# Four graph layers on one core: chunk 0's graph attention woven into the attention iterations, and another order of work at both ends

## The reference

```python
x = x + attention0(h, adj)        # 8 heads of 32, softmax over the neighbours, with biases
x = x + attention1(h, adj)        # the same without biases in q, k, v; o + layernorm(o) * gamma + beta
x = x + graph_attention(h, adj)   # hw = h W; e = leaky(s1_i + s2_j) * adj; softmax; elu(att hw + beta hw)
x = x + recurrence(h, adj)        # three steps of a gated unit:
#   a = adj h; z = sigmoid(a W3 + h U3); r = sigmoid(a W4 + h U3)
#   hv = tanh(a W5 + (r h) U5); h = (1 - z) h + z hv
```

## Time and profile before

| | us |
|---|---|
| median of 3 runs | 1524.75 (1520.08 to 1526.09) |
| the profiled execution, its own time | 1525.95 |
| its span in the trace | 1524.2 |
| TensorE busy | 1463.7 |
| VectorE busy | 1244.6 |
| ScalarE busy | 991.5 |
| GpSimd busy | 534.8 |

### The profile page before, as it was taken

One profiled execution on the slowest core, in us unless ns is written; L12 is line 12 of the kernel. 1 busy time (PEld: TensorE's weight loads), 2 busy tenths in 40 slices (PEclk: granted clock), 3 DMA queues, 4 the chain that ended last, 5 costly groups with the idle time before them and its releaser, 6 DMA issues.

```text
span 1524.2 us, 45691 instructions
## 1 busy us (share of the span) xinstructions
PE 1463.7 (96%) x18840; PEld 1233.9 (81%) x18840; DVE 1244.6 (82%) x2510; ACT 991.5 (65%) x1792; POOL 534.8 (35%) x622
## 2 busy tenths in 40 slices
PE   5899999899899998799999999999999999999997
PEld 4789989799798887588888888888888887888885
DVE  4777888888899999788888788888888888888676
ACT  4666667577677776666666666666666666666553
POOL 2676777567777887411111111111101111111000
PEclk9999999999999999899999999999999999999998
DMA  8200000012322235100000000000000000000000
GB/s 263 85 3 0 0 0 1 7 26 44 58 55 55 55 64 78 29 1 1 29 2 2 30 1 1 30 1 1 30 1 1 30 1 1 29 2 1 29 1 28
DMA packets 36827, 40.96 MB, mean 27 GB/s; under 512 B 11856, under 2 KB 31824, under 8 KB 36688
## 3 DMA queue, kind: packets, MB, share of 16 engines
q0 software_dynamic: 4608, 16.78, 5.9%
q1 hardware_dynamic: 32080, 22.10, 4.9%
HBM read 13.71 MB, written 8.39 MB: 14 GB/s over the span
## 4 chain that ended last, share of the span: by engine, by line
PE 87%; DVE 7%; POOL 2%; ACT 2%; issue 2%; DMA 0%; DVEq 0%; POOLq 0%; ACTq 0%
PE ring L99 40%; PE scores L99 27%; PE scores L1589 3%; PE ring L1408 3%; PE scores L1372 2%; PE ring L1448 2%; PE ring L1629 2%; PE ring L1419 1%; PE ring L1573 1%; PE ring L1701 1%; PE ring L1531 1%; POOL s L534 1%; PE ring L1542 1%; DVE total L993 1%; DVE stats L955 1%
## 5 line engine op out<-in xcount | busy, mean ns | idle before, releaser
L534 POOL TENSOR_TENSOR s<-s,mx 128x512 f32<-128x512 f32 x128 | 137.4, 1092 | 49.4 <-DVE mx L989 49.4
L540 POOL TENSOR_TENSOR s<-s,rtotal 128x512 f32<-128x512 f32 x128 | 131.4, 1064 | 35.9 <-DVE rtotal L995 35.7
L600 POOL TENSOR_TENSOR r_var_eps<-r_mean_var,eps 128x4 f32<-128x4 f32 x16 | 8.1, 509 | 377.1 <-DVE r_mean_var L1146 377.1
L684 ACT ACTIVATE s<-s 128x512 f32<-128x512 f32 x128 | 78.3, 643 | 75.1 <-POOL s L534 75.1
L1275 DVE TENSOR_TENSOR rhp_lo<-r,rhp_hi 128x1024 fp32r<-128x1024 f32 x48 | 58.8, 1226 | 72.8 <-ACT rhp_hi L865 72.8
L984 DVE SCALAR_TENSOR_TENSOR s<-scores,mask 128x512 f32<-128x512 f32 x128 | 87.2, 681 | 35.4 <-PE scores L1372 35.4
L884 ACT ACTIVATE hv<-scores,bias 128x512 f32<-128x512 f32 x96 | 66.2, 689 | 58.0 <-PE scores L99 58.0
L847 ACT ACTIVATE r<-r,bias_half 128x512 f32<-128x512 f32 x96 | 64.4, 717 | 59.6 <-DVE r L1249 59.6
L858 ACT ACTIVATE later_w<-ring 128x512 f32<-128x512 f32 x64 | 34.8, 595 | 99.9 <-PE ring L1629 99.9
L696 ACT ACTIVATE pT<-ring 128x512 f32<-128x512 f32 x128 | 66.1, 602 | 45.4 <-PE ring L1408 45.4
L989 DVE TENSOR_REDUCE mx<-s 128x8 f32<-128x512 f32 x128 | 87.9, 686 | 4.4
(11 more groups left out here) (288 smaller groups left out, 5108.6 us busy)
## 6 DMA issues: line engine op xcount, KB each, us to landing
x<-beta_less_one POOLq DMA_DIRECT2D x16, 512.0 KB, 4.7
x<-o POOLq DMA_DIRECT2D x16, 512.0 KB, 6.6
...
```

The source lines that it names most:

```text
L534: pool.tensor_tensor(sr, sr, mx[:, r, :].unsqueeze(2).to_broadcast([P, CT * 2, N]), ALU.subtract).then_inc(s_shifted, 1)
L540: pool.tensor_tensor(sr, sr, rtotal[:, r, :].unsqueeze(2).to_broadcast([P, CT * 2, N]), ALU.mult).then_inc(p_ready, 1)
L684: act.activation(s[:, par, r, :, :, :], s[:, par, r, :, :, :], ACT.Exp).then_inc(p_exp, 1)
```

## The change

**Opening.** TensorE makes 48 transposes of ident into high[0] before anything else and 10 more in iteration -1 (`keep_clock`). In iteration 0 TensorE does the row transposes of chunk 1 ahead of the scores of chunk 0, and the product for out_bias between q and k; ScalarE and VectorE get written out bodies (`first_body`) in which the split of wo, the statistics of chunk 2 and the exponentials change places; GpSimd's norm comes behind the four subtractions.

**Weave.** The loop over iterations 20 to 29 is written out (WEAVE = 22). The graph attention of chunk 0 is put, link by link, into iterations 22 to 30: beta_ident and statistics in 22, norm and rows in 23, transposes and split in 24, products in 25 and 26, s2, e and the shift in 27, attention and attT in 28, aggregate and the additions into x in 29, the statistics for the recurrence in 30. It has buffers of its own (`first_rows`, in later_w and w_ext).

**Transition.** Only chunk 1's graph attention is left behind iteration 30. Chunk 0's rows of the recurrence are entered between its products, and the first half step (`begin`) is mixed: u3 of chunk 0, then o_products(T), attT of chunk 1, values(T), adjacency, aggregate, o_products(T + 1), w4, w3, enter(1), w5. ScalarE's and VectorE's programs follow the same order; several parts of the second layer's end (o_normalise, final_sum, o_stats) come later than before.

**Close.** In the last half step w5 and u5 are made in pieces of 256 columns in four banks (`close_w5`, `close`), r times h and its parts per half ahead of z_sum (`close_rh`), the update in four pieces, and the last store in two of 256 KB.

The diff, cut to its core (new buffer places, the renamed arguments and the counterparts of the same order on ScalarE are left out):

```diff
@@ -125,6 +125,7 @@
...
     with Phase(nc) as ctx:
...
@@ -387,10 +403,8 @@
                 body(j * 2 + 4, 0, 0)
             for i in range(CHUNKS - 3, CHUNKS + 4):
                 body(i, i % 2, 0)
-            with eng.Fori(0, (CHUNKS - 6) // 2) as j:
-                body(j * 2 + CHUNKS + 4, 0, 1)
-                body(j * 2 + CHUNKS + 5, 1, 1)
-            body(T - 2, 0, 1)
+            for i in range(CHUNKS + 4, T - 1):
+                body(i, i % 2, 1)
...
                     sp.wait_ge(left, c * 2 + 2)
                     sp.dma_start(dst[:, bass.ds(c * CT, CT), :], x[:, bass.ds(c * CT, CT), :]).then_inc(stored, 16)
-                sp.wait_ge(stored, 16 * CHUNKS)
+                for q in range(2):
+                    cut = slice((CHUNKS - 1) * CT + 2 * q, (CHUNKS - 1) * CT + 2 * q + 2)
+                    sp.wait_ge(left, (CHUNKS - 1) * 2 + q + 1)
+                    sp.dma_start(dst[:, cut, :], x[:, cut, :]).then_inc(stored, 16)
+                sp.wait_ge(stored, 16 * (CHUNKS + 1))
...
                 def body(i, par, lay):
-                    norms(i, par, lay)
+                    first = isinstance(i, int) and i == 0
+                    if not first:
+                        norms(i, par, lay)
                     if isinstance(i, int) and i == T - 2:
...
                         shift(i, par, 3)
+                    if first:
+                        norms(i, par, lay)
+                    if isinstance(i, int) and i == WEAVE + 1:
+                        norm(gn, 0, 0)
...
                 def norm(ln, c, q):
...
+                def first_body():
+                    split_high(1)
+                    act.wait_ge(w_loaded[3], 16)
+                    act.activation(parts[0]["o"].hi[:], stage[:, 3, :, :], ACT.Copy).then_inc(w_hi_ready, 1)
+                    act.activation(bv_rows[:], col_bias[:, 2, :].unsqueeze(2).to_broadcast([P, FT, P]), ACT.Copy)\
+                        .then_inc(bv_spread, 1)
+                    copy_projection(1, 0, qT, 0)
+                    exponential(0, 0, 0)
+                    copy_projection(1, 1, kT, 0)
+                    for r in range(1, R):
+                        exponential(0, 0, r)
+                    copy_v(1, 1)
+                    normalise(0, 0, 0)
+
...
+                def first_body():
+                    rows_low(1)
+                    for r in range(R):
+                        mask_and_max(0, 0, r, 0)
+                    dve.wait_ge(bias_product, 1)
+                    dve.tensor_tensor(out_bias[0][:], out_bias[0][:], scores[:, 0, 0:D], ALU.add)\
+                        .then_inc(bias_ready, 1)
+                    x_stats(2, 0)
+                    for r in range(R):
+                        sums(0, 0, r)
+                    split_low(0, [3])
+
+                def woven(i):
+
+                    if i == WEAVE:
+                        dve.tensor_scalar(beta_ident[:], ident[:], g_beta[:, 0:1], None, ALU.mult)\
+                            .then_inc(beta_ident_ready, 1)
+                        rows_stats(gn, 0, x_final)
+                    if i == WEAVE + 5:
+                        graph_leaky(0)
+                        dve.memset(first_rows.att[:], 0.0).then_inc(first_att_cleared, 1)
+                    if i == WEAVE + 6:
+                        dve.wait_ge(beta_ident_ready, 1)
+                        copy_attT(0, high, 0)
+                    if i == WEAVE + 7:
+                        graph_positive(0, high, 2)
+
+                def woven_last(i):
+                    if i == WEAVE + 7:
+                        graph_negative(0)
+                    if i == WEAVE + 8:
+                        recurrence_stats(0)
+
...
+                def close_rh(s):
+                    n = s.n + 1
+                    old = h[s.me]
+                    for m in range(FT):
+                        dve.wait_ge(r_done, s.n * FT + m + 1)
+                        dve.scalar_tensor_tensor(r[:, m, :], r[:, m, :], 1.0, old[:, m, :], ALU.add, ALU.mult)\
+                            .then_inc(rh_done, 1)
+                    for m in range(FT):
+                        dve.wait_ge(rh_hi_ready, n + m)
+                        dve.tensor_tensor(rhp.lo[:, m, :], r[:, m, :], f32(rhp.hi[:, m, :]), ALU.subtract)\
+                            .then_inc(rh_lo_ready, 1)
...
                 def begin(s):
-                    graph_positive(1, ring, 0)
+                    graph_positive(1, high, 2)
                     agg_low(0)
                     graph_negative(1)
                     recurrence_stats(1)
+                    take_first(T + 1, 1, 1)
+                    take_out(T - 1, 1, 1, 1)
                     r_sum(0)
+                    o_stats(T, 0, 1)
                     z_sum(0)
+                    dve.wait_ge(o_stats_ready, CHUNKS - 1)
+                    o_stats(T + 1, 1, 1)
+                    enter(1, 1)
+                    final_sum(T, 0, 1)
                     rows_stats(gn, 2)
+                    final_sum(T + 1, 1, 1)
                     final_sum(T + 2, 0, 1)
-                    enter(1, 1)
                 def half(s):
                     n = s.n
...
+                def woven(i):
+
+                    if i == WEAVE + 2:
+                        pe.wait_ge(s_masked, i * R + 2)
+                        graph_rows(0, high)
+                    if i == WEAVE + 3:
+                        pe.wait_ge(gw_lo_ready, 1)
+                        pe.wait_ge(s_masked, (i + 1) * R)
+                        graph_product(0, 0, high, 2)
+                        graph_product(0, 1, high, 2)
+                    if i == WEAVE + 4:
+                        pe.wait_ge(s_masked, (i + 1) * R)
+                        graph_product(0, 2, high, 2)
+                        graph_product(0, 3, high, 2)
+                    if i == WEAVE + 5:
+                        pe.wait_ge(s_masked, i * R + 2)
+                        graph_s2(0, high, 0)
+                    if i == WEAVE + 6:
+                        pe.wait_ge(s_masked, i * R + 1)
+                        graph_attT(0, high, 0)
+                    if i == WEAVE + 7:
+                        pe.wait_ge(s_masked, (i + 1) * R)
+                        graph_aggregate(0, high, 2)
+
                 def later_weights(i):
                     if i == CHUNKS - 1:
                         pe.wait_ge(halves_added, 1)
@@ -1475,19 +1660,40 @@
                         weight_transposes(3)
                         weight_transposes(4)
+                def keep_clock(bank, times):
+
+                    for _ in range(times):
+                        pe.transpose(bank[:, 0:P], ident[:], ident[:])
...
                     if exists(i):
                         scores_piece(i)
                     if exists(i - 1):
                         p_transposes(i, par)
-                    if exists(i + 1):
+                    if exists(i + 1) and not first:
                         x_transposes(i)
+                    if isinstance(i, int) and i == -1:
+                        keep_clock(high[:, 0, :], 10)
                     if exists(i - 2):
                         o_products(i, lay)
                     if exists(i - 1):
                         values(i, par)
                     if isinstance(i, int):
                         later_weights(i)
+                        woven(i)
                     if exists(i + 1):
...
                 def begin(s):
                     pe.wait_ge(h0_lo_ready, FT)
-                    pe.wait_ge(x_done, T * 2)
                     for m in range(FT):
-                        product(pe, ring[:, 2 + m, :], columns(wT["u3"], m), moving(hp[0])).then_inc(hu_ready, 1)
-                    graph_aggregate(1, ring, 0, hw_next)
-                    pe.wait_ge(e_sum, 2)
-                    pe.wait_ge(hw_copied, 2 * FT)
+                        product(pe, high[:, m, :], columns(wT["u3"], m), moving(hp[0])).then_inc(hu_ready, 1)
+                    o_products(T, 1)
+                    graph_attT(1, high, 2)
+                    values(T, 0)
+                    pe.wait_ge(hu_copied, FT)
                     pe.wait_ge(adj_loaded, 32)
-                    adjacency(r_hn[0])
+                    adjacency(r_hn_first)
+                    graph_aggregate(1, high, 2)
+                    o_products(T + 1, 1)
                     pe.wait_ge(agg_lo_ready, FT)
-                    pe.wait_ge(x_plus_pos, 4)
                     for m in range(FT):
                         product(pe, ring[:, m, :], columns(wT["w4"], m), moving(agg)).then_inc(r_ready, 1)
                     for m in range(FT):
                         product(pe, high[:, m, :], columns(wT["w3"], m), moving(agg)).then_inc(z_ready, 1)
+                    pe.wait_ge(x_done, T * 2)
+                    enter(1, r_hn[1])
+                    pe.wait_ge(x_plus_pos, 4)
                     for m in range(FT):
                         product(pe, high[:, 2 + m, :], columns(wT["w5"], m), moving(agg), ends=False)
```

(57 more changed lines are left out.)

324 lines of the change are left out of this document (205 added, 119 removed).

## The result

The changed kernel took 1521.44 us against 1523.68 for the kernel before: a ratio of 0.9984, with a 95% interval of 0.9977 to 0.9991. That is 2.2 us faster where 14.6 were forecast. The gain is clear of zero, and by the 0.5% of the prediction it is no change.

A forecast was written before the change was run, and what follows sets the result against it. TensorE, busy 96% of the span, was taken as the bound. Terms -8.5 + 6.1 + 4 + 6 - 19 - 3.2 = -14.6, and 1.2 from profiled run to median, took 1525.95 to 1510 us; range 1498 to 1523.

The forecast's parts named there:

- transition: Last scores to second half step's u5: moving chunk 0's attention out and reordering saves 19 us (13 to 25).
- VectorE's room and the new waits: Iterations 22 to 30: woven VectorE work fits overall but not per iteration, so TensorE waits: +4 us (0 to +8).
- The opening: Start and iterations 0 and 1: idle transposes and a new order save 8.5 us (4 to 11).
- The clock term: Start: idle transposes bring TensorE's clock up before the first projection, -2.1 us (bounds +1.7 and -2.4).
- The moved work: Iterations 22 to 30: chunk 0's graph attention, moved out of the transition, adds 6.1 us on TensorE.
- Late code in the written-out iterations: Iterations 22 to 30: straight code must be fetched and sometimes comes late, +6 us (0 to 30).
- The close: Last half step: halves of 256 columns and a store in two pieces save 3.2 us (2 to 5).
- Rival 2: Iterations and transition: waits in the weave give back the transition's gain, -1.6 us in sum, 1523; chance 0.15.
- Rival 1: Iterations 22 to 30: code comes in time and woven steps fit VectorE's room, no +6 or +4: 1500; chance 0.2.
- Rival 3: Values stage of iterations 22 to 30: late code nearly every time, +30 in place of +6, 1534; chance 0.07.
- Rival 4: Opening: clock not up or falls again, softmax holds iteration 1; -4 instead of -8.5, 1515; chance 0.08.
- The prediction's own signs: Wrong if the transition gains under 13 us, or if holes of the code are none or over five.

The follow-up runs named there:

- clock_alone: Kernel before plus only the 58 idle TensorE transposes (48 at the start, 10 ahead of the first projection): 1517.20 us, ratio 0.9960.
- no_clock: Changed kernel without its 58 idle transposes: 1521.53 us, ratio 0.9981 to the kernel before.
- scale_late: Changed kernel with GpSimd's multiplication by gamma of iteration 28 behind its four normalise steps: 1518.53 us, ratio 0.9970 to the kernel before.
- ends_unroll: Kernel before with new opening and close and the loop over iterations 20 to 29 written out, nothing woven: 1508.08 us, ratio 0.9898.
- ends: Kernel before with the new opening and close only, loop kept, nothing woven: 1508.36 us, ratio 0.9900.
- pad30: Kernel before plus 30 idle transposes (60 instructions) ahead of the first real one: 1531.02 us, ratio 1.0041.

## Why the prediction was wrong

Two steps failed, and the larger is the **transition**: -19 forecast, -8.0 measured, 11 us too much, where the whole sum missed by 10.4. The order worked out left out GpSimd's queue, and with it a wait that the prediction has nowhere, 11.3 us for the graph rows of chunk 2; and a hole of late code stood there, 4.1 us. The second is the price of **VectorE's room and the new waits** in the iterations, +4 forecast, 13.2 us of waits measured. It doesn't show in the total, since +6 for late code and 5.5 us in iterations 20 and 21 fell the other way: from iteration 2 to the last scores 16.1 us were forecast and 14.4 measured. That these two are near each other is luck.

- **The opening, -8.5 forecast, -7.4 measured.** Its size was right, its terms less: iteration 0 -8.7 (forecast -8.0), iteration 1 +2.7 (+1.6), the start -1.4 (-2.1). The clock term alone gave nothing with the old order (clock_alone) and 0.8 to 2.7 us with the new one.
- **The moved work, +6.1** (its own terms add up to 6.0). From its start to that of what follows, the woven work took 6.3 us on TensorE, so the price was right. TensorE's busy time rose by 7.8 us (165.5 for 157.7), and that isn't 6.1 and a rest. Iteration 23 has none of the woven TensorE work, and behind its wait of 2.7 us it ran at a clock of 0.92; in no_clock it has the same wait, and the clock stayed:

```profile
425.44:446.59 21.15, 18.43 (x353) 16.64 (x352) 19.58 (x57) 13.49 (x26) 15.40 (x19) 0.92 0.28 52
...
428.51:448.82 20.31, 17.56 (x353) 15.48 (x353) 18.74 (x57) 13.38 (x26) 14.53 (x18) 1.00 0.28 54
```

That is 0.9 us for the low clock. Iteration 30 shows 1.05 in the same way (18.44 busy at 0.92, 17.39 in scale_late at 1.00, both behind a wait of 2.1), and 28 about 2 by my estimate (20.2 for 17.7 before, less its woven transposes). The clock thus cost about 4 us, a term that the prediction doesn't have in the iterations, and they took in about 2 of the 6 us of moved work.
- **VectorE's room and new waits, +4 (0 to +8).** Measured are 13.2 us of waits. The prediction did name the place (22, and 27 to 30) and the queue (masks, hT_lo), and then priced it by the room of the whole stretch, 13.4 to 15.4 us into 16.8. The room is per iteration, about 1.2 + what TensorE gets. It also priced the attention product at "0.9 to 2.9" from a row that had its explanation beside it in the trace, GpSimd's multiplication, and took the leaky part at 0.42, a value measured without such a one:

```profile
600.83 2.99 POOL L566 TENSOR_TENSOR o_n<-o_n,gamma 128x1024 f32<-128x1024 f32 x1
```

- **Late code in the written-out iterations, +6.** Wrong: written-out code costs 1 us here (159.0 for 157.9), and ends_unroll equals ends. Of the 25 packets that the instruction queue brings there, none left a hole of 0.5 us. Elsewhere they did: pad30 shows 2.4 us holes, and after one of 4.1. What the prediction missed is that late code was a matter of position here, so that an edit moved holes elsewhere: -5.5 in iterations 20 and 21, -1.1 before them, and +4.1 in the transition. The +6 was therefore wrong in place and in sign: the sum of the three is about -2.5.
- **The transition, -19 (-13 to -25), -8.0 measured.** The new order by hand was right for TensorE and VectorE, and left out GpSimd's queue: the norm of chunk 2 behind two multiplications. Mended, it gave 6.7; without the hole in the adjacency product it gives 5.0 to 5.5. Without both it is 54.4 for 73.5: **-19.1**. That it meets the forecast to 0.1 us is in part luck: TensorE still waits 4.2 us for the graph rows of chunk 2, which the forecast doesn't have.
- **The close, -3.2, -3.8 measured.** Right.
- **The rivals.** Rival 2 (1523) is what came in time, and its mechanism, VectorE's queue in the iterations, in kind; its numbers were +17 for waits and code and -13 for the transition, against 13.2 of waits and -8. Rival 1 had the code in the iterations right and the waits wrong. Rival 3 did not occur; a change of position alone cost 7.4 us (pad30), in another place. Rival 4 did not occur either: the opening gave 7.4 us, and its clock was granted in full in iteration 0 (1.00).
- **The prediction's own signs.** It called itself wrong if the transition gained under 13 us or if no hole of the code stood in iterations 22 to 30. Both came: 8.0 us, and none.

The sum by the measured terms: -7.4 - 1.1 - 5.5 + 21.0 - 8.0 + 0.6 - 3.8 = -4.2 in the profiled executions.

What stays open: why the holes in iterations 20 and 21 need the loop as well as the position; what remains of the waits for hT_lo in iterations 25, 28 and 30; and how much VectorE's fullness costs with the stalls gone.
